# Four-layer cross-attention: PE's program padded to whole pages of instructions, and softmax units cut another way

## The reference

```python
# layer 0: 16 heads of 64, inner width 1024, a bias on four context columns
q, k, v = x @ Wq, ctx @ Wk, ctx @ Wv
probs = softmax(einsum('bhqd,bhkd->bhqk', q, k) * 64 ** -0.5 + col_bias)
x = x + (probs @ v).reshape(B, 64, 1024) @ Wo + bo
# layers 1 to 3: 16 query heads of 8, 4 key heads of 8
xn = x * rsqrt(mean(x * x) + 1e-5) * norm_w
q, k, v = xn @ wq, ctx @ wk, ctx @ wv
attn = softmax(einsum('btgrd,bsgd->bgrts', q, k) / sqrt(8))
x = x + einsum('bgrts,bsgd->btgrd', attn, v) @ wo
```

## Time and profile before

| | |
|---|---|
| median of 3 runs | 1511.65 us (1511.49 to 1513.16) |
| the profiled execution's own time | 1509.35 us |
| its span, first to last instruction | 1507.5 us |
| granted TensorE clock, mean over the span | 0.99 |
| busy: PE, weight loads, DVE, ACT, POOL | 97%, 77%, 71%, 73%, 51% |
| instructions fetched for PE | 3.10 MB in 189 packets |

### The profile page before, as it was taken

The page is one execution under the profiler, slowest core; times in us unless marked ns, Lnnn a source line. Parts: engine busy times, 40 slices in busy tenths (PEclk is TensorE's granted clock), DMA queues, the critical chain, the costliest instruction groups (busy, mean ns, idle before and its releaser), DMA issues.

```text
span 1507.5 us, 56267 instructions
## 1 busy us (share of the span) xinstructions
PE 1462.3 (97%) x23872; PEld 1167.3 (77%) x23872; DVE 1072.9 (71%) x2291; ACT 1107.7 (73%) x2529; POOL 773.0 (51%) x881
## 2 busy tenths in 40 slices
PE   7999999999999999999999999999999999999875
PEld 5787878887878877877887877877777787878763
DVE  1467777777777777777777777777777777777875
ACT  3577777787777777777787777777777787777764
POOL 3345555445555445555445555445555455555643
PEclk9999999999999999999999999999999999999987
DMA  5100000100000100000001001110000100000000
GB/s 153 28 21 14 24 21 24 26 20 21 25 24 22 26 22 19 25 24 21 26 16 25 25 21 25 25 27 15 24 22 23 26 16 17 18 14 18 17 11 8
DMA packets 57178, 36.92 MB, mean 24 GB/s; under 512 B 16864, under 2 KB 55776, under 8 KB 56928
## 3 DMA queue, kind: packets, MB, share of 16 engines
q1 hardware_dynamic: 56032, 33.22, 8.6%
q10 hardware_dynamic: 896, 0.10, 0.0%
HBM read 16.49 MB, written 4.19 MB: 14 GB/s over the span
## 4 chain that ended last, share of the span: by engine, by line
PE 93%; DVE 2%; issue 1%; SPq 1%; ACT 1%; POOL 1%; DMA 0%; POOLq 0%; ACTq 0%
PE bank L398 15%; PE bank L457 15%; PE bank L390 15%; PE bank L475 8%; PE bank L425 7%; PE bank L448 6%; PE bank L494 6%; PE bank L437 4%; PE bank L466 4%; PE bank L357 3%; PE bank L500 3%; PE bank L481 3%; PE bank L413 2%; PE bank L406 2%; DVE st L657 1%
## 5 line engine op out<-in xcount | busy, mean ns | idle before, releaser
L341 POOL TENSOR_TENSOR E<-E,st 128x512 f32<-128x512 f32 x512 | 533.3, 1042 | 667.4 <-DVE st L668 667.4
L665 DVE TENSOR_REDUCE st<-E 128x8 f32<-128x512 f32 x512 | 341.1, 666 | 194.7 <-ACT E L573 143.9
L573 ACT ACTIVATE E<-E,inv 128x256 f32<-128x256 f32 x768 | 347.9, 507 | 14.9 <-DVE E L661 7.6
L578 ACT COPY E<-bank 128x512 f32<-128x512 f32 x512 | 286.4, 587 | 58.3 <-PE bank L457 57.7
L457 PE MATMUL bank<-ident,E 128*128 128x128 f32 x2048 | 289.1, 277 | 11.5 <-POOL E L341 11.4
L657 DVE TENSOR_REDUCE st<-bank 128x8 f32<-128x512 f32 x384 | 251.6, 677 | 64.2 <-PE bank L448 60.6
L457 PEld LDWEIGHTS bank<-ident,E 128*128 128x128 f32 x2048 | 243.7, 143 | 49.8 <-POOL E L341 14.6
L661 DVE TENSOR_TENSOR E<-bank,st 128x512 f32<-128x512 f32 x384 | 256.1, 674 | 0.0
L390 PE MATMUL bank<-cT,wk 128*128 128x256 f32 x1024 | 247.5, 385 | 2.7 <-ACT cT L522 2.3
L398 PE MATMUL bank<-wv,cT 128*128 128x512 f32 x512 | 247.0, 605 | 0.0
L390 PEld LDWEIGHTS bank<-cT,wk 128*128 128x128 f32 x1024 | 186.5, 192 | 27.5 <-ACT cT L522 2.7
(11 more groups left out here) (62 smaller groups left out, 1701.8 us busy)
## 6 DMA issues: line engine op xcount, KB each, us to landing
KB<-K SPq DMA_DIRECT2D x1536, 8.0 KB
cin<-in_ctx SPq DMA_DIRECT2D x32, 256.0 KB, 3.7
xin<-in_x SPq DMA_DIRECT2D x32, 128.0 KB, 2.6
out<-xN SPq DMA_DIRECT2D x32, 128.0 KB, 2.0
wk<-in_L_xattn_Wk SPq DMA_DIRECT2D x2, 512.0 KB, 8.0
wv<-in_L_xattn_Wv SPq DMA_DIRECT2D x2, 512.0 KB, 9.8
wq<-in_L_xattn_Wq SPq DMA_DIRECT2D x1, 512.0 KB, 9.2
wo<-in_L_xattn_Wo SPq DMA_DIRECT2D x1, 512.0 KB, 5.3
```

The costliest lines, as they stand in the source:

```text
L341: e.tensor_tensor(E3, E3, wide(stat[s][u][:, 16:24]), ALU.mult).then_inc(g_nrm.sem, 1)
L573: m = e.activation(E[s][u][:, 256 * p:256 * p + 256], E[s][u][:, 256 * p:256 * p + 256], ACT.Exp, scale=inv[s][:, p:p + 1])
L578: e.copy(E[s][u][:, :], bank_of["t", g, l, u][:, :]).then_inc(a_et.sem, 1)
L665: e.tensor_reduce(stat[s][u][:, 8:16], heads(E[s][u][:, :]), AX, ALU.add).then_inc(d_sum.sem, 1)
```

## The change

The five tables are new. In `PE_TIME` the two `pv0` units of a group now follow each other, and so do the two layer-0 `s` units. The period in the tables is 44.42 instead of 44.96; it is a number for the order alone.

PE's program gets waits that are met already: `PE_FIRST` = 86 calls at its start, which make 43 instructions, and `PE_FILL` = 12 ahead of each `k` unit, which make six, 24 a group. With them a group has 1536 instructions of PE instead of 1512.

In the small layers a unit of the softmax is now a pair of sequences and two of the four head sets: unit u takes pair u // 2 and sets 2 (u % 2) and 2 (u % 2) + 1, so it reads half of each of two neighbouring banks. The four score banks become one tensor `scores`. exp is issued once a unit, over 512 columns. `pv` finds its operands accordingly.

```diff
+PE_FIRST = 86
+PE_FILL = (12, 12, 12, 12)
-PERIOD = 44.96
+PERIOD = 44.42
 PE_TIME = {
...
-    "pv0": {0: (161.41, 163.5)},
+    "pv0": {0: (145.15, 146.13)},
...
-        banks = [ctx.enter_context(nc.psum_tensor(f"bank{i}", [128, 512], F32)) for i in range(8)]
+        scores = ctx.enter_context(nc.psum_tensor("scores", [128, 4, 512], F32))
+        banks = [ctx.enter_context(nc.psum_tensor(f"bank{i}", [128, 512], F32)) for i in range(4)]
...
+        def pairs(ap):
+            return ap.rearrange("p (r h k) -> p r h k", r=2, k=64)
...
-                bank_of["scores", g, l, unit] = banks[i]
+                if l == 0:
+                    held[i] = ("add", g, l, unit)
+                    scores_of[g, l, unit] = scores[:, i, :]
+            for unit in units if l else ():
+                p, r = unit // 2, unit % 2
+                held[at[2 * r + p]] = ("sub", g, l, unit)
+                scores_of[g, l, unit] = scores[:, at[2 * r]:at[2 * r] + 2, 256 * p:256 * p + 256].rearrange(
+                    "p r (h k) -> p r h k", k=64)
+            bank_of[st] = at
...
+            for _ in range(PE_FIRST):
+                e.wait_ge(l_ident.sem, 16)
             w.wait_ge(l_ident, "ident")
...
                     w.wait_ge(l_wk[u // 2], u // 2)
+                    for _ in range(PE_FILL[u]):
+                        e.wait_ge(l_ident.sem, 16)
...
-                                n, c = 256 * (b // 2) + 128 * gp + 64 * (b % 2), 96 * (l - 1) + 32 * gp
+                                n, c = 256 * (r % 2) + 128 * gp + 64 * (b % 2), 96 * (l - 1) + 32 * gp
                                 m = e.matmul(bank[32 * r:32 * r + 32, 64 * b:64 * b + 64], VBg[:, b, c:c + 32],
-                                             E[s][r][:, n:n + 64], start=(gp == 0), stop=(gp == 1))
+                                             E[s][2 * (b // 2) + r // 2][:, n:n + 64], start=(gp == 0), stop=(gp == 1))
...
-                        for p in range(NP):
-                            m = e.activation(E[s][u][:, 256 * p:256 * p + 256], E[s][u][:, 256 * p:256 * p + 256],
-                                             ACT.Exp, scale=inv[s][:, p:p + 1])
-                        m.then_inc(a_exp.sem, 1)
+                        e.activation(E[s][u][:, :], E[s][u][:, :], ACT.Exp, scale=inv[s][:, u // 2:u // 2 + 1]
+                                     ).then_inc(a_exp.sem, 1)
...
-                    e.tensor_tensor(heads(E[s][u][:, :]), heads(bank_of["scores", g, l, u][:, :]),
-                                    wide(stat[s][u][:, 0:8]), ALU.subtract).then_inc(d_sub.sem, 1)
+                    e.tensor_tensor(pairs(E[s][u][:, :]), scores_of[g, l, u],
+                                    stat[s][u][:, 0:8].rearrange("p (r h a) -> p r h a", r=2, a=1).to_broadcast(
+                                        [128, 2, 4, 64]), ALU.subtract).then_inc(d_sub.sem, 1)
```

More of the change, by code:

```diff
@@ L27 @@
 SCALE8 = float(np.float32(1.0) / np.sqrt(8).astype(np.float32))
-PERIOD = 44.96
+PE_FIRST = 86
+PE_FILL = (12, 12, 12, 12)
+PERIOD = 44.42
 PE_TIME = {
     "cT": {0: (0,)},
[L36 to L46, removed]
-    "pv0": {0: (161.41, 163.5)},
[L48 to L52, removed]
+    "k": {0: (77.62, 50.36, 63.43, 91.76)},
+    "v": {0: (66.68, 96.73, 83.01, 84.95)},
+    "k3": {0: (93.48,)},
+    "v3": {0: (113.26,)},
+    "xT": {0: (91.48,)},
+    "q0": {0: (116.35, 118.58, 117.72, 121.19)},
+    "s": {0: (124.92, 125.9), 1: (159.73,), 2: (191.58,), 3: (222.65,)},
+    "t": {0: (142.87, 143.31, 144.17, 144.61),
+          1: (177.26, 176.82, 176.38, 175.95),
+          2: (208.72, 209.16, 209.6, 208.28),
+          3: (243.94, 242.85, 243.29, 237.05)},
+    "pv0": {0: (145.15, 146.13)},
+    "wo0": {0: (148.7,)},
+    "xt": {1: (154.88,), 2: (185.35,), 3: (218,)},
+    "q": {1: (157.25,), 2: (188.17,), 3: (219.94,)},
+    "pv": {1: (179.28,), 2: (212.71,), 3: (247.52,)},
+    "wo": {1: (183.19,), 2: (215.78,), 3: (250.54,)},
@@ L53 @@
 }
 ACT_TIME = {
[L55 to L74, removed]
+    "cT": {0: (1.97,)},
+    "k": {0: (80.87, 53.49, 65.35, 93.67)},
+    "v": {0: (68.79, 98.64, 85.42, 86.86)},
+    "k3": {0: (94.53,)},
+    "v3": {0: (114.71,)},
+    "xT": {0: (92.98,)},
+    "q0": {0: (117.91, 119.63, 118.77, 122.81)},
+    "exp": {0: (134.68, 136.85, 136.29, 134.12),
+            1: (167.73, 166.52, 168.45, 170.22),
+            2: (196.41, 200.98, 195.52, 202.84),
+            3: (237.34, 234.66, 230.47, 229.13)},
@@ L75 @@
+    "et": {0: (143.57, 144.06, 144.83, 145.32),
+           1: (178.05, 177.56, 177.07, 176.58),
+           2: (209.47, 209.96, 210.45, 208.98),
+           3: (244.91, 243.54, 244.42, 238.05)},
+    "pv0": {0: (146.52, 147.51)},
+    "x2": {1: (157.27,), 2: (184.34,), 3: (217,)},
+    "xt": {1: (155.29,), 2: (185.77,), 3: (218.41,)},
+    "q": {1: (158.14,), 2: (188.97,), 3: (220.64,)},
+    "pv": {1: (180.43,), 2: (213.86,), 3: (248.67,)},
 }
 DVE_TIME = {
-    "add": {0: (141.49, 143.93, 149.28, 146.82)},
@@ L78 @@
[L78 to L95, removed]
+    "add": {0: (126.1, 131.21, 130.52, 128.27)},
+    "max": {0: (129.84, 132.98, 131.89, 129.16),
+            1: (163.72, 163.04, 164.4, 160.88),
+            2: (193.41, 196.34, 192.73, 197.44),
+            3: (231.88, 230.53, 225.83, 223.8)},
@@ new lines @@
+    "sum": {0: (136.31, 139.84, 138.75, 135.63),
+            1: (168.62, 167.83, 169.5, 171.41),
+            2: (198.8, 201.86, 206.18, 203.73),
+            3: (238.51, 235.54, 233.45, 231.2)},
+    "rcp": {0: (138.55, 140.59, 141.48, 138.35),
+            1: (173.39, 169.3, 171.21, 172.5),
+            2: (200.17, 202.95, 207.27, 205.98),
+            3: (239.87, 236.63, 234.81, 233.25)},
+    "wo0": {0: (152.59,)},
+    "ssq": {1: (158.11,), 2: (191.79,), 3: (221.42,)},
+    "sub": {1: (165.76, 165.07, 166.45, 167.14),
+            2: (195.65, 198.11, 194.76, 199.48),
+            3: (234.12, 232.56, 229.64, 226.51)},
@@ L96 @@
+    "wo": {1: (183.85,), 2: (216.51,), 3: (251.28,)},
 }
 POOL_TIME = {
[L98 to L104, removed]
+    "xb": {0: (119.74,)},
+    "sub": {0: (131.49, 134.69, 132.65, 130.44)},
+    "nrm": {0: (139.67, 140.87, 141.91, 138.63),
+            1: (173.82, 169.57, 171.48, 172.77),
+            2: (200.44, 204.02, 207.54, 206.25),
+            3: (240.15, 237.7, 235.09, 233.52)},
@@ L105 @@
+    "ms": {1: (158.6,), 2: (192.28,), 3: (222.54,)},
 }
 SP_TIME = {
[L107 to L110, removed]
+    "cT": {0: (84.65,)},
+    "kr": {1: (95.07,), 2: (151,), 3: (162,)},
+    "xT": {0: (194.92,)},
+    "st": {0: (261.84,)},
 }
@@ L209, in wide @@
             return ap.rearrange("p (h a) -> p h a", a=1).to_broadcast([128, 8, 64])
-        bank_of, before = {}, {}
+        def pairs(ap):
+            return ap.rearrange("p (r h k) -> p r h k", r=2, k=64)
+        bank_of, before, scores_of = {}, {}, {}
         held, n = [None] * 4, 0
@@ L220, in xattn_kernel @@
             for i, unit in zip(at, units):
-                held[i] = ("add" if l == 0 else "sub", g, l, unit)
-                bank_of["scores", g, l, unit] = banks[i]
+                if l == 0:
[7 more added lines that the diff above has]
+            bank_of[st] = at
         held, n = [None] * 4, 0
@@ L227, in xattn_kernel @@
             before[st] = [held[i] for i in at if held[i]]
-            bank_of[st] = [banks[4 + i] for i in at] if st[0] == "pv0" else banks[4 + at[0]]
+            bank_of[st] = [banks[i] for i in at] if st[0] == "pv0" else banks[at[0]]
             for i in at:
@@ L428, in tensor_program @@
                 elif kind == "s" and l == 0:
-                    bank = [bank_of["scores", g, 0, 2 * u + h2] for h2 in range(2)]
                     w.wait_ge(a_ev, *[("q0", g, 0, i) for i in range(4)])
@@ L436, in tensor_program @@
                                     lo, n, j, c = 64 * h2, 128 * u + 64 * b2, 2 * jj + par, 128 * jj + 64 * b2
-                                    m = e.matmul(bank[h2][64 * par:64 * par + 64, c:c + 64],
+                                    m = e.matmul(scores[64 * par:64 * par + 64, bank[h2], c:c + 64],
                                                  QT[s][lo:lo + 64, j, n:n + 64], KTg[lo:lo + 64, j, n:n + 64],
@@ L447, in tensor_program @@
                                 lo, b = 32 * r, 2 * p + b2
-                                m = e.matmul(bank_of["scores", g, l, r][64 * b2:64 * b2 + 64, 256 * p:256 * p + 256],
+                                m = e.matmul(scores[64 * b2:64 * b2 + 64, bank[r], 256 * p:256 * p + 256],
                                              QT[s][lo:lo + 32, 0, 64 * b:64 * b + 64],
@@ L646, in vector_program @@
                         w.wait_ge(p_ev, ("pv", g - NS, 3, 0))
-                    e.tensor_tensor(heads(E[s][u][:, :]), heads(bank_of["scores", g, l, u][:, :]),
+                    e.tensor_tensor(heads(E[s][u][:, :]), heads(scores_of[g, l, u]),
                                     bias[:, :].rearrange("p (a k) -> p a k", a=1).to_broadcast([128, 8, 64]), ALU.add
```

(2 more changed lines are left out.)

## The result

| | before | changed |
|---|---|---|
| median | 1512.23 us (4 runs, 1511.49 to 1513.16) | 1532.52 us (4 runs, 1530.30 to 1537.00) |
| profiled span | 1507.5 us | 1528.6 us |

The ratio is 1.0138, 95% interval 1.0110 to 1.0165: the change made the kernel slower by 1.4%. The forecast was 1515, with a range from 1489 to 1522.

What follows compares the result with a forecast made beforehand. PE was taken to bound the kernel, with work in flight for 1462.3 of 1507.5 us. Span: 1507.5 - 13 - 7.5 + 24 + 0.4 = 1511.4; median 1515.5, called 1515 (+0.2%), range 1489 to 1522.

Steps and rivals of the forecast that it cites:

- Order: New unit order on PE, fewer small-tile runs and paired units: -0.41 us a group, 31 groups, -13 us.
- Padding: PE groups filled to 1536 instructions, six pages, so page turns stand still and the sliding stops go: -7.5 us.
- The fixed page: Page turning in wo each group: 2.45 us of work, next page ready after 3.3; 0.86 lost, 28 groups, +24 us.
- 24 waits a group: Met waits ahead of each k unit, 51 ns each, covered by work PE has already queued: 0.
- Start: 43 wait instructions at the start of PE's program, mostly covered by later idle time: +0.4 us (0 to +1.5).
- Units: Recut softmax units in the small layers: some 4 us less ACT a group, PE waits for none in mid-run: 0.
- Tail and head: Tail, from the last v3 unit on: same work within 1 us, idle time left as is (within 3 us).
- Rival 3: The padding waits ahead of k units show on top of the fixed page's stop: from 1524 to 1549; chance 0.05.
- Rival 1: The 2.45 us page is on time, or turns lie elsewhere, nothing lost: median 1491.5, -1.3%; chance 0.28.

Runs made afterwards that it cites:

- the best run: Changed kernel without waits at the start, the 24 a group ahead of three k units, none behind pv and xT: 1491.28 us, ratio 0.9865 to before.
- the run with 102: Changed kernel with PE_FIRST = 102 instead of 86, so every page turn comes 8 instructions earlier: 1536.82 us, ratio 1.0165 to the kernel before.

## Why the prediction was wrong

The mechanism and the place were right; the sum was 17 us of span short. By its parts:

1. *Order*: said -0.41 a group, measured -0.516 (44.979 to 44.463 in the best run), so -16 instead of -13. The 0.10 is in the two pairs: I took a pair as 0.98 + 1.09, but it is 0.98 + 1.04 (757.50 to 759.53 above is 2.03).
2. *Padding*, -7.5: right. In the padded kernels no stop slides through mid-run.
3. *The fixed page*, **the step that failed**: said 0.86 a group, 28 groups, +24; measured 1.13, +31.6. The work was right, 2.44 for 2.45 (the expectations above have 2.34, with 0.11 for wo's first pass, which takes 0.21). The ready time was not: 3.47 on the mean, not 3.3, which is 0.17 of the difference. The other 0.10 I had left out: the pass behind the stop takes 0.22 (715.28 to 715.50), undisturbed 0.11, as the run without waits ahead shows in its timeline from 516.0 on:
```profile
515.80 0.28 PE L520 MATMUL bank<-wos,QT 128*128 128x128 f32 x1
515.91 0.59 PE L419 MATMUL bank<-wv,cT 128*128 128x512 f32 x1
```
Both errors are small, but the loss is a difference of two large terms. My mean of 3.3 came from nine stops, and this time is no constant of the kernel: its mean was 3.21 in the run with 102.
4. *24 waits a group*, said 0: wrong. I read 51 ns an instruction and it is 0.11 of the sequencer, 0.64 for six. At three places that is covered; behind pv and xT it costs 0.11 a group (44.576 without waits ahead, 44.463 in the best run), 31 groups, +3.5. The changed kernel loses another 0.16 to 0.19 at the same xT in 11 of its 28 groups, +1.8. The run without waits ahead has the same waits and does not lose it, so they alone are not the cause; a page turns five passes ahead of that xT, and why this costs something in some groups stays open.
5. *Start*: first matmul at 8.50 instead of 4.28, first k at 10.26 instead of 9.39: +0.9, said +0.4. Again the spacing of the waits.
6. *Units*: nothing in mid-run, right within what a run can tell. One exp takes 739 ns, not 631, which I had read from a unit with a constant scale.
7. *Tail and head*: said 0. Two single stops in the head, at a pv0 pair (57.0 and 97.6 us), are new: +3.1. They are page turns too; I had looked only at the repeating ones. The lower clock behind the first of them is another +1.6. Some 2 us more lie in the first and last groups and are not traced to a row.

Sum: 1507.5 - 16 - 7.5 + 31.6 + 3.5 + 1.8 + 0.9 + 3.1 + 1.6 = 1526.5, and 2.1 unexplained to 1528.6.

Rival 3 (the waits show, on top of part 3, from 1524), to which I gave 0.05, comes nearest: the waits do show at one place. But they cost 0.11 there, not 0.31, and the time lies in its range mainly through the longer stop and the head.

Rival 1 (the page is on time) gave 1491.5 and named turns 8 instructions later, a page of 3.6 us, as one way to it. The run with 8 instructions less has a page of 3.74 and measured 1498.5, those with the turns farther away 1496.4 and 1491.3. So the sum without the stop was good to a few us, and so was the side on which the page of 2.45 us lies; what was mis-sized is the stop.

The Trainium skill ("Runtime: NRT & Kernel Launch", Instruction fetch mechanics) says that the next block is fetched while the current one runs and that a crossing is mostly hidden. The runs limit this: in the two without waits ahead every crossing between 100 and 1350 us is hidden, and no page there lasts under 5.9 us; the page of 2.44 us, turned onto in short passes, was not hidden in any of 28 groups.

## What to carry to other kernels

Where an engine's program is unrolled and has no slack, count its instructions between page turns and add up the work of the shortest page: here one that was turned onto in a run of short passes needed 3.0 to 4.05 us until the next was there, and what it has less is a stop. A table that packs short instructions together makes such pages itself. Padding a loop to whole pages makes the turns repeat, which is worth as much as the phase that is then chosen, for good or ill; try several phases, since here 8 instructions were worth 34 us. Put met waits where long instructions stand ahead, and price them by their spacing in the trace, not by their duration.

## What was not expected of the hardware

- Waits that are met cost PE's sequencer 0.11 us each from start to start, while the trace gives each 51 ns (24 in 2.5 us; 42 from 3.7 to 8.2 at the start).
- PE goes on 1.37 us behind the end of the page's packet (126 stops, 1.21 to 1.61), not at once.
- Behind short passes the packet starts 0.5 to 1.6 us behind PE's turn (runs with 70 to 102 waits ahead); shortly behind a full unit it started up to 0.84 ahead of it, and a page of 2.0 us then passed without a stop.
- A pass of 0.11 takes 0.22 behind a stop.
- Idle times of 1.8 to 1.9 us lowered the granted clock at 21 of 30 places, to 0.52 in the windows above, and so did 1.55 and 1.25 with a few passes between; the single stops in wo, up to 1.45, did not.
